# A cross-attention block and a recurrent block on one core: group 0's feed-forward prepared earlier, first loads by quarters, queries moved to the border, adds and state columns on other engines

## The reference

```python
# block 1, cross attention (16 heads of 32)
q = LN(x) @ q_w + q_b;  k = ctx @ k_w + k_b;  v = ctx @ v_w + v_b
h = x + softmax(q k^T / sqrt(32)) v @ cproj_w + cproj_b
h = h + gelu(LN(h) @ fc_w + fc_b) @ proj_w + proj_b          # inner size 2048
# block 2, recurrence (32 heads of 16)
xa = LN(h);  sx = shift(xa) - xa
xxx = tanh((xa + sx*maa_x) @ maa_w1) @ maa_w2                # five low-rank mixes
xk, xw, xv, xr, xg = xa + sx * (maa_stack + xxx)
w = exp(-exp(time_decay + tanh(xw @ td_w1) @ td_w2));  r, k, v = xr@Wr.T, xk@Wk.T, xv@Wv.T
g = silu(xg @ Wg.T)
for t: out_t = sum_i r_t[i]*(u[i]*k_t[i]*v_t + s[i]);  s[i] = k_t[i]*v_t + w_t[i]*s[i]
x1 = h + (group_norm(out)*gn_w + gn_b) * g @ Wo.T
xc = LN(x1);  sx2 = shift(xc) - xc
y = x1 + sigmoid((xc+sx2*mix_r)@Wfr.T) * (relu((xc+sx2*mix_k)@Wfk.T)**2 @ Wfv.T)
```

## Time and profile before

| | before |
|---|---|
| median of 3 runs | 1736.65 us (1735.44 to 1737.56) |
| profiled execution, its own time | 1739.64 us |
| its span | 1736.7 us |
| busy TensorE matmul, weight load | 1621.9 us (93%), 870.2 us (50%) |
| busy VectorE | 1178.6 us (68%) |
| busy ScalarE, GpSimd | 666.3 us (38%), 281.0 us (16%) |
| mean granted TensorE clock | 0.973 |
| chain that ended last | PE 69%, DVE 21%, issue 5%, ACT 3% |

### The profile page before, as it was taken

The page is one execution under the profiler, slowest core; times in us unless marked ns, Lnnn a source line. Parts: engine busy times, 40 slices in busy tenths (PEclk is TensorE's granted clock), DMA queues, the critical chain, the costliest instruction groups (busy, mean ns, idle before and its releaser), DMA issues.

```text
span 1736.7 us, 21228 instructions
## 1 busy us (share of the span) xinstructions
PE 1621.9 (93%) x7976; PEld 870.2 (50%) x7976; DVE 1178.6 (68%) x1850; ACT 666.3 (38%) x1551; POOL 281.0 (16%) x377
## 2 busy tenths in 40 slices
PE   6999999799999999999999999999899998987968
PEld 3555555445555454555555555555445454433423
DVE  1232200366998895669997955799899677999741
ACT  2456511225666223246662222466431226222111
POOL 1100000122211001231210011221100142036020
PEclk9999999899999999999999999999999998999989
DMA  8011112143111223351112333510132342222221
GB/s 273 3 30 37 36 49 94 56 123 108 47 38 61 76 74 132 110 153 39 46 32 83 97 126 101 162 46 9 48 100 86 119 139 88 79 93 78 69 91 45
DMA packets 76787, 142.24 MB, mean 82 GB/s; under 512 B 16672, under 2 KB 26784, under 8 KB 76688
## 3 DMA queue, kind: packets, MB, share of 16 engines
q1 hardware_dynamic: 61664, 105.51, 19.1%
q0 software_dynamic: 11776, 31.70, 6.2%
q10 hardware_dynamic: 3248, 3.70, 0.7%
HBM read 117.03 MB, written 23.86 MB: 81 GB/s over the span
## 4 chain that ended last, share of the span: by engine, by line
PE 69%; DVE 21%; issue 5%; ACT 3%; ACTq 1%; DMA 1%; POOL 0%; SPq 0%; DVEq 0%; POOLq 0%
PE bank L344 40%; PE bank L678 8%; PE bank L532 6%; DVE C L1426 5%; PE bank L386 4%; PE bank L378 3%; PE bank L538 2%; PE bank L398 2%; DVE C L1435 2%; DVE YB L1444 2%; DVE sm L1363 1%; DVE C L1596 1%; DVE C L1418 1%; PE bank L644 1%; PE bank L629 1%
## 5 line engine op out<-in xcount | busy, mean ns | idle before, releaser
L1426 DVE TENSOR_TENSOR_SCAN C<-XA,C 128x896 f32<-128x896 f32 x112 | 228.8, 2043 | 4.2 <-ACT XA L1108 1.0
L1363 DVE CUSTOM_DVE_ANT_0 sm<-bank,maskb 112x375 f32<-112x375 f32 x256 | 124.4, 543 | 139.4 <-PE bank L378 139.0
L344 PE MATMUL bank<-ctx_t,Wk 128*128 128x375 f32 x512 | 198.4, 513 | 12.7 <-DMA Wk<-in_wk 11.3
L344 PE MATMUL bank<-SX,ring 128*128 128x448 f32 (+2 forms) x544 | 195.9, 519 | 4.1 <-issue 4.1
L344 PE MATMUL bank<-Wv,ctx_t 128*125 128x512 f32 x384 | 180.9, 596 | 0.4 <-ACT C L1074 0.4
L386 PEld LDWEIGHTS bank<-ident,sm 112*125 112x125 f32 x768 | 124.6, 191 | 105.6 <-ACT sm L1089 45.0
L1095 ACT ACTIVATE probT<-bank 125x336 f32<-125x336 f32 x256 | 114.1, 446 | 160.5 <-PE bank L386 159.1
L1089 ACT ACTIVATE sm<-sm,nm 112x375 f32<-112x375 f32 x256 | 153.3, 599 | 3.3 <-DVE nm L1363 3.3
L344 PEld LDWEIGHTS bank<-SX,ring 128*128 128x128 f32 x544 | 100.5, 190 | 95.5 <-issue 92.5
L532 PE MATMUL bank<-HT,ring 128*128 128x448 f32 x384 | 146.3, 539 | 0.0
L386 PE MATMUL bank<-ident,sm 112*125 112x112 f32 x768 | 125.9, 273 | 8.7 <-ACT probT L1095 8.7
(11 more groups left out here) (185 smaller groups left out, 2408.4 us busy)
## 6 DMA issues: line engine op xcount, KB each, us to landing
ring<-in_stream SPq DMA_DIRECT2D x64, 1024.0 KB, 5.3
ctx_t<-in_ctxT SPq DMA_DIRECT2D x16, 750.0 KB, 4.7
rkw_scratch<-HT POOLq DMA_DIRECT2D x32, 224.0 KB, 5.0
rkw<-rkw_scratch POOLq DMA_DIRECT2D x24, 224.0 KB, 3.1
HT<-in_x SPq DMA_DIRECT2D x16, 224.0 KB, 5.1
X<-in_x SPq DMA_DIRECT2D x16, 224.0 KB, 6.1
rkw_scratch<-YB POOLq DMA_DIRECT2D x16, 224.0 KB, 3.3
v_scratch<-HT POOLq DMA_DIRECT2D x16, 224.0 KB, 5.5
```

Source lines behind the costliest of these rows:

```text
L344: last_ = nc.tensor.matmul(out_ap, pairs[k][0], pairs[k][1], start=(k == 0), stop=(k == len(pairs) - 1))
L1363: nc.vector.tensor_tensor_reduce(out=sm[0:LQ, slot, :], in0=tile(name)[0:LQ, 0:LK], in1=maskb[:, n % 2, :], scale=-SCALE, scalar=3.0e38, o ...
L1426: own.step(nc.vector.tensor_tensor_scan(out=part, data0=wrep[:, i % 2, :], data1=part, initial=0.0, op0=ALU.mult, op1=ALU.add))
```

## The change

The order in which ready groups get their feed-forward part becomes 0, 2, 1, 3 (`LAST`). The keys of row 0 are loaded by quarters, the context by SyncE and the weight by ScalarE, and computed quarter by quarter in four banks; the small weights of block 2 are issued by SyncE behind the first ring pieces and not by ScalarE. In the first MLP the fc product's first 336 columns stand where the queries of group 1 stood, and these queries go between the transposes of the first border. Group 0's statistics, norm and columns are made in the last MLP and its mixes behind the last but one group norm; in `pre(3)` group 2 (`k = 1`) takes group 0's place, and its mixes leave the recurrence. `AHEAD` is moved forward. GpSimd's `last_add` goes to VectorE's `last_out`; `last_stds` handles four rows at once. From step 4 on the state column is copied by ScalarE behind `repeat_decays`. In the tail the table of the square root is loaded ahead, the gate is made and used by quarters, and norm and columns alternate on ScalarE.

```diff
-LAST = [2, 0, 1, 3]
+LAST = [0, 2, 1, 3]
...
-         12: [("ln", 2)], 14: [("fk", 2, 0), ("fk", 2, 1)], 15: [("fk", 2, 2), ("fk", 2, 3)],
-         RS: [(kind, 2, at) for kind in ("fr", "fv") for at in range(4)]}
+AHEAD = {0: [("fk", 0, at) for at in range(4)] + [("fr", 0, 0), ("fr", 0, 1)], 1: [("fr", 0, 2), ("fr", 0, 3)],
+         2: [("fv", 0, 0), ("fv", 0, 1)], 3: [("fv", 0, 2), ("fv", 0, 3)],
+         4: [("fk", 1, 0), ("fk", 1, 1)], 5: [("fk", 1, 2), ("fk", 1, 3)],
+         6: [("fr", 1, 0), ("fr", 1, 1)], 7: [("fr", 1, 2), ("fr", 1, 3)],
+         8: [("ln", 2)], 9: [("fv", 1, 0), ("fv", 1, 1)], 10: [("fv", 1, 2), ("fv", 1, 3)],
+         11: [("fk", 2, 0), ("fk", 2, 1)], 12: [("fk", 2, 2), ("fk", 2, 3)], 13: [("fr", 2, 0), ("fr", 2, 1)],
+         RS: [("fr", 2, 2), ("fr", 2, 3)] + [("fv", 2, at) for at in range(4)]}
...
+            def mlp_first():
...
+                first = [wide() for e in range(E)]
...
+                columns(0, 0, cut)
+                evacuated(pe, ("RD", n))
+                k = opened(SC[0])
+                closed(out_proj(k), ("WC", n), k)
+                for e in range(1, E):
+                    columns(e, 0, cut)
+                k = opened(SC[1])
+                pe.wait_ge(xn_ready["ln2"], n + 1)
+                rows_to_cols(k, xn[:, 1, :], ("TY", n))
+                evacuated(pe, ("TY", n))
+                for e in range(E):
+                    closed(columns(e, cut, T), ("FC", 0, e), first[e])
+                mlp_rest(0, E)
...
+                    if g == NG - 1 and m == 0:
+                        last_cols(0)
...
             def border(g):
                 if g == 0:
+                    pre_cols(g, 0)
                     for b in range(GB):
-                        pre_cols(g, b)
+                        evacuated(pe, ("TX", GB + b))
+                    query(1, 0)
+                    pre_cols(g, 1)
+                    pre_cols(g, 2)
+                    query(1, 1)
+                    pre_cols(g, 3)
+                    query(1, 2)
+                    query(1, 3)
...
-            pe.wait_ge(ctx_in[0], 16)
-            pe.wait_ge(wk_in, 16)
-            for e in range(E):
-                k = narrow()
-                closed(keys(k, 0, e), ("K", 0, e), k)
+            k0 = [opened(SC[e]) for e in range(E)]
+            for c in range(E):
+                pe.wait_ge(ctx0_in[c], 16)
+                pe.wait_ge(wk_in[c], 16)
...
+            def last_stds(k):
...
+                nc.gpsimd.tensor_scalar(vare["post"][:, at], mv["post"][:, at, 1], EPS, None, ALU.add
...
+                nc.gpsimd.tensor_tensor(rstd["post"][:, at], vare["post"][:, at],
+                                        half[0:LQ, :].to_broadcast([LQ, GB]), ALU.pow
...
+                nc.gpsimd.tensor_tensor(shift[:, at], mv["post"][:, at, 0], rstd["post"][:, at], ALU.mult
...
+                nc.gpsimd.tensor_scalar(shift[:, at], shift[:, at], -1.0, None, ALU.mult).then_inc(shift_ready, GB)
...
+                if p == NG - 1 and i >= 4:
+                    act.wait_ge(summed, i - 3)
+                    nc.scalar.activation(S_last[i % 4][:, :, 0], s0[:, i, :], ACT.Copy).then_inc(first_set, 1)
...
+                        if g == NG - 1 and m == 0:
+                            last_norm(0, e, e + 1)
+                            if e == E - 1:
+                                last_cols(0)
...
                 if g == NG - 1:
-                    last_norm(0)
-                    last_cols(0)
+                    last_norm(1)
                 for e in range(0 if g == NG - 2 else E - (g < NG - 1)):
+                    if g == NG - 1 and e == 2:
+                        last_cols(1)
...
+                        if i == 0:
+                            last_keys(0)
+                        elif i in (2, 3):
+                            last_gate(0, 2 * (i - 2), 2 * (i - 2) + 2)
+                        elif i in (7, 8):
+                            last_keys(1, 2 * (i - 7), 2 * (i - 7) + 2)
                         elif i in (9, 10):
...
+                            last_gate(1, 2 * (i - 9), 2 * (i - 9) + 2)
+                        if i == 9:
                             last_norm(2)
-                        elif i == 14:
+                        elif i == 10:
                             last_cols(2)
-                    last_keys(2)
+                        elif i in (13, 14):
+                            last_keys(2, 2 * (i - 13), 2 * (i - 13) + 2)
                     last_gate(2)
+                    nc.scalar.activation(ahead[:, :], epsc[:, :], ACT.Sqrt)
                     group_std(p)
-                    last_norm(NG - 1)
-                    last_cols(NG - 1)
+                    for b in range(GB):
+                        last_norm(NG - 1, b, b + 1)
+                        if b > 0:
+                            last_cols(NG - 1, b - 1, b)
+                    last_cols(NG - 1, GB - 1, GB)
...
+                    if not last or i < 4:
+                        own.step(nc.vector.tensor_copy(S[:, :, 0], s0[:, i, :]))
...
+                    if last and i >= 4:
+                        dve.wait_ge(first_set, i - 3)
...
-                    if k == NG - 1:
-                        evacuated(dve, name)
-                        nc.vector.tensor_tensor(last_rows(k, b), last_rows(k, b), RR[b], ALU.add).then_inc(ffn_ready, 1)
+                    evacuated(dve, name)
+                    nc.vector.tensor_tensor(last_rows(k, b), last_rows(k, b), RR[b], ALU.add).then_inc(ffn_ready, 1)
...
+                    if g == NG:
+                        own.settle()
+                        nc.vector.tensor_tensor(C[0][:, e, :], C[0][:, e, :], GT[:, e, :], ALU.mult).then_inc(og_ready, 1)
...
+                    if g == NG - 1:
+                        units(p, IN_STEPS, IN_STEPS + UNITS)
+                        last_stats(0)
+                        units(p, IN_STEPS + UNITS, RS * UNITS)
...
                         group_norm(p)
+                        if g == NG - 1:
+                            last_mixes(0)
                         gate(g)
...
-                        if i == 2:
-                            last_mixes(1)
-                        elif i in (7, 8):
-                            last_out(0, 2 * (i - 7), 2 * (i - 7) + 2)
-                        elif i == 11:
+                        if i in (5, 6):
+                            last_out(0, 2 * (i - 5), 2 * (i - 5) + 2)
+                        elif i == 8:
                             last_stats(2)
-                        elif i in (13, 14):
-                            last_out(1, 2 * (i - 13), 2 * (i - 13) + 2)
-                        elif i == 15:
+                        elif i in (11, 12):
+                            last_out(1, 2 * (i - 11), 2 * (i - 11) + 2)
+                        elif i == 10:
                             last_mixes(2)
```

More of the change, by code:

```diff
@@ L149, in build @@
         epsc = sb("epsc", [P, 1])
+        ahead = sb("ahead", [P, 1])
         ctx_t = sb("ctx_t", [P, 2, E, LK])
@@ L273, in build @@
         wrep_ready = sem("wrep_ready")
+        first_set = sem("first_set")
         scan_step = sem("scan_step")
@@ L520, in mlp, with columns, mlp_rest @@
                        ("FC", g, 0), first)
+                mlp_rest(g, 1)
+            def mlp_first():
+                n, w, cut = GB - 1, weights(0, ("fc", 0)), (GB - 1) * LQ
+                for b in range(GB - 1):
+                    evacuated(pe, ("TY", b))
+                first = [wide() for e in range(E)]
+                def columns(e, lo, hi):
+                    return product(bank[first[e]][:, lo:hi], [(w[:, c, e * P:(e + 1) * P], YT[:, c, lo:hi])
+                                                              for c in range(E)])
+                columns(0, 0, cut)
[11 more added lines that the diff above has]
+                mlp_rest(0, E)
+            def mlp_rest(g, made):
                 for m in range(4):
                     channels_out([("FC", g, 4 * m + e) for e in range(E)], weights(g, ("fc", m)), YT,
-                                 lo=1 if m == 0 else 0)
+                                 lo=made if m == 0 else 0)
                     piece_done(g, ("fc", m))
@@ L694, in pre @@
                 by_blocks(3, {0: lambda: low_rank(4)})
-                if g == NG - 1:
-                    last_cols(0)
                 if g != NG - 2:
-                    w, late = weights(g, PRE_P[3]), g < NG - 1
+                    w, names = weights(g, PRE_P[3]), [("P", g, 4, e) for e in range(E)]
                     pe.wait_ge(mix_ready, g * MIXES + MIXED[4])
-                    channels_out([("P", g, 4, e) for e in range(E)], w, mixed[4], any_bank, hi=E - late)
-                    if not late:
+                    if g < NG - 1:
+                        channels_out(names, w, mixed[4], any_bank, hi=E - 1)
+                    else:
+                        channels_out(names, w, mixed[4], any_bank, hi=2)
+                        last_cols(1)
```

(26 more changed lines are left out.)

129 lines of the change are left out of this document (66 added, 63 removed), and 5 rows, old and new, of the table AHEAD.

## The result

| | before | after |
|---|---|---|
| median | 1736.77 us (1735.44 to 1737.56, 4 runs) | 1723.53 us (1720.45 to 1726.61, 4 runs) |
| ratio | | 0.9925 [0.9905, 0.9944] |
| profiled execution, its own time | 1739.64 us | 1722.52 us |
| its span | 1736.7 us | 1720.4 us |
| mean granted clock | 0.973 | 0.978 |

The kernel is 13.2 us faster; 14.3 was forecast (1722.3 as median). The page of after: busy times by engine, then the engines' shares of the chain that ended last.

What follows compares the result with a forecast made beforehand. TensorE was taken to carry most of the chain, VectorE about a fifth. Terms -7.6 - 8.7 + 4.0 + 9.5 - 2.3 - 9.2 gave -14.3: 1725.3 us profiled, 1722.3 as median; range 1709 to 1731.

Steps and rivals of the forecast that it cites:

- Start: Kernel start: key weight by quarters lands at 5.0 us, keys end at 18.2, values begin at 20.4; -7.6 us.
- Small loads in front of nothing needed: Start: small loads moved to SyncE stand in front of nothing needed before the first border; no size of its own.
- First MLP and border: First MLP -8.7 us, fc columns replacing queries; first border +4.0, queries filling it and W1 taking 4.3 instead of 6.25.
- Last MLP: Last MLP: preparing group 0 there makes ScalarE wait for the shift and TensorE stop 5.6 us; +9.5 us.
- Rival A: Last MLP: GpSimd slips through between VectorE's operations, so the term is +3 and the time 1715.8; chance 0.20.
- Rival D: Last MLP: shift ready only at 1292, +18.5 us on the forecast, 1740.8, slower than before; chance 0.05.
- Pre stage to the last sum: Last pre stage and recurrence, paced by VectorE: seven parts, (a) to (g), together -2.3 us, bounds -10 to +3.
- (a): Pre stage: norm, table load, SiLUs and columns on ScalarE delay VectorE's mixes, so the recurrence starts +2.5 us later.
- Tail: Tail: earlier square-root table -4.1, round trip +0.4, gate by quarters -3.7, earlier columns -1.8; together -9.2 us.
- The 4.1: Tail: the square root's table comes earlier and fr is shorter by two, cutting VectorE's idle before its reciprocal; -4.1 us.
- Rival B: Start gives only -3, later loads slowing the quarters and TensorE slow for all 32 records; 1726.9; chance 0.15.
- C: Last MLP and recurrence: new waits equal what the moved parts free; 1737.3, no difference; chance 0.05.

Runs made afterwards that it cites:

- the start in whole loads: The changed kernel with context and key weight each in one load on SyncE's queue, keys block by block in two banks; 1728.66 us, ratio 0.995.
- the kernel in which VectorE stands: The changed kernel with VectorE, behind its four statistics for group 0, waiting until GpSimd has made the shift; 1719.85 us, ratio 0.9904.
- the kernel with both edits: The changed kernel with group 0's norm one quarter later in the last MLP and VectorE's mixes of k=2 one step later; 1712.45 us, ratio 0.9865.

## Why the prediction was right

**Start** (-7.6, measured -8.0 on the mean). The landing and the sum held, 4.42 for 5.0. The reason was incomplete: I gave the bank wait to the banks' number, and it was ScalarE's queue of loads, as the start in whole loads shows (no bank wait with two banks). And 0.7 of the 8.0 is chance: the key products took 13.20 in before's one trace and 12.5 in the mean of the twelve with quarters. "Small loads in front of nothing needed" looked only at where they went, not at where they had stood.

**First MLP and border** (-4.7, measured -3.8, and 3.8 by undoing it). The first fc product ends 8.7 earlier on the mean, as forecast. Its first part, put at 2.3, takes 2.50 in seven of twelve traces and 4.16 to 4.19 in five (granted clock 0.57 in after), behind the same 1.62 of idle in all of them. The mis-sized term is the border: +4.9 on the mean for the +4.0 forecast. W1 runs at full clock in every one (4.04), but the first query there takes 4.2 to 5.8 where a warm one takes 3.

**Last MLP** (+9.5, measured +9.4). Term by term: wait 5.6 forecast and 5.35 measured, slow restart 2.0 and 3.0, transposes 1.7 and 1.70, bank 0.3 and 0.48, VectorE's wait for the repeat 1.9 and 1.83. TensorE's part adds to 10.5, and its last transposes come 10.8 later; the first sum comes only 10.0 later in this trace, since before it had waited 0.8 longer, for VectorE's gate. Rival A (GpSimd slips through) fell with the 2.64, 1.31 and 2.02, and the kernel in which VectorE stands shows their cause. Rival D needed a shift at 1291 and had no place, since ScalarE's wait was 14.49 for the 14 forecast.

**Pre stage to the last sum** (-2.3, measured -0.9). From the recurrence's start to the last product I forecast -3.05 and the change is -3.2; the parts undone one at a time give +2.35 for the adds (8.1 less 5.8), +0.97 for the columns, and 7.5 for the new wait. (a) holds for the ScalarE chain: from its first norm in the pre stage to VectorE's mixes takes 10.80 instead of 8.41, +2.4 for +2.5. But the stage from the MLP's end to there is 3.9 longer, and the sum has no term for the rest. The rows of TensorE, before and after, place it in the products with the low-rank mixes (`sm,mw`) and the one behind them:

```profile
1383.56 1.16 PE L644 MATMUL bank<-sm,mw 32*128 32x112 f32 x32
1386.67 3.25 PE L678 MATMUL bank<-C,ring 128*128 128x448 f32 x8 [1.95 <-DVE C L1611]
```

```profile
1377.55 0.36 PE L695 MATMUL bank<-sm,mw 32*128 32x112 f32 x1
1378.85 1.16 PE L695 MATMUL bank<-sm,mw 32*128 32x112 f32 x31 [0.93 <-issue]
1381.79 4.94 PE L729 MATMUL bank<-C,ring 128*128 128x448 f32 x8 [1.79 <-DVE C L1701]
```

TensorE stops for 0.93 where the trace shows no wait, and the product behind it runs at less granted clock (0.65 in after, 1.00 before). In twelve of the thirteen traces without before's the stop is 0.80 to 1.35 long, and the product behind it takes 3.25 to 6.07. With the queries of group 1 back it is 0.22 and the product takes 3.25, and there the whole stage takes 92.27: +2.3, what (a) alone gives. What makes the stop stays open.

**Tail** (-9.2, measured -8.6). Right in sum, wrong in its parts. The 4.1 is there, but not from the square root ahead. The trace gives it to the sigmoids: the last one ended 22.9 behind the last product before and ends 14.5 behind it now; no run put the two back. The gate by quarters gives 2.8 and not 3.7, since 0.9 of before's 11.1 was the GpSimd add beside its product; the rest, 2.6 where 1.8 was forecast, includes it. The round trip cost 1.0 instead of 0.4: the stores of k=2 leave earlier once VectorE does the adds, and meet it.

Rival B (a start worth less) and C (no net) fell with the stages above. The median would not have decided all of it: the interval of the ratio runs from 1720 to 1727 us and leaves out A (1715.8), but not B (1726.9). Against B stands the start in the trace.

## What to carry to other kernels

When work is moved ahead on one engine, write down what is queued behind its first wait: here 3 us of norms cost 9.4 and could be had for about 3, one quarter later, once the operand was long ready. Put a consumer one step behind its producer rather than behind the same step, and keep bulk stores off the moment at which a round trip is waited for. To credit a part of a change, take it out alone, and look at the same stage in several traces before a microsecond gets an owner: the start and the tail here had the right sum and in part the wrong owner, and one slow product in the first MLP was chance.

## What the runs showed of the hardware

- ScalarE is held by the loads that it issues: two issues of small loads took 5.51 and 4.44 us where its others took 0.4 to 1.7, its table load began at 18.62, 0.09 behind the last of them, and its first arithmetic at 19.92. On SyncE, in the changed kernel, the same two took 2.69 and 1.71.
- Small GpSimd operations on 112x4 elements take 1.05, 0.20 and 0.26 us alone and 2.64, 1.31 and 2.02 beside VectorE's products and sums of 128x1792; VectorE's operations stretch beside GpSimd's adds in turn (4.08 to 5.91, 2.02 to 2.98). The Trainium skill ("SBUF — State Buffer", Who interferes with whom) says that whoever issues first holds the shared ports; both directions are seen here.
- TensorE's granted clock differs between executions of the same code. From 30 to 90 us TensorE is busy for 56.0 us in both traces shown here, with 267 matmuls at a granted clock of 0.91 and with 314 at 1.00 (columns: stretch, length, busy us and count of PE, PEld, DVE, ACT, POOL, clock, DMA share, GB/s):

```profile
30.00:90.00 60.00, 56.00 (x267) 30.96 (x266) 12.80 (x47) 27.61 (x75) 4.47 (x6) 0.91 0.13 37
```

```profile
30.00:90.00 60.00, 56.00 (x314) 31.26 (x313) 15.29 (x56) 30.07 (x82) 4.47 (x6) 1.00 0.19 55
```

  The first is the kernel with both edits, the second the one without the square root ahead; attention of group 0 took 172.22 and 167.45. In fourteen traces this stage took one of four lengths, near 167.4, 169.1, 170.7 and 172.2, whatever the edit, while the VectorE-bound recurrence repeated within 0.04 us.
- Four stores of 224 KB lengthened y's round trip from 9.7 to 11.8 us in the kernel with both later parts.
